# P times V in two attentions: the matmul moves the head's own 64 or 16 columns of V instead of 128

## The chip, the core and the metric

The kernel runs on one NeuronCore of a Trainium2 chip. The metric is the device time of one execution in microseconds (us); ns are nanoseconds. Both kernels compute the same function of the same inputs.

## What is computed

Eight layers follow each other on a residual of 4 batches x 512 tokens x 256 channels: a Mamba layer, a mixture of experts, a rotary attention, the same mixture, an attention with sinks, a second mixture, a latent attention, and the second mixture again. Cut to the three attentions, where `ln` is a layer norm:

```python
x = x + rotary(ln(x))   # 16 heads of 16, causal:           att = softmax(q k^T / 4);   y = att v
x = x + sinks(ln(x))    # 32 query heads, 8 kv heads of 64, softmax over all 512 keys and one
                        # sink logit, keys of the last 64 positions masked;             y = w v
x = x + latent(ln(x))   # 16 heads of 128 over one latent k, causal, v is k itself;     y = att k
```

What the change touches is the product `att v` (P times V) of the rotary and the sinks attention.

## The kernel before

One function, `attention`, writes all three attentions from a description `a`: `a.D` is the head size (16 rotary, 64 sinks, 128 latent), `a.HG` = 4 the query heads of a group, `a.G` the groups (4, 8, 4), `KW` the width of all V heads (256, 512, 128). Names of tiles begin with `ra_`, `sa_` and `la_`.

The work of a group in a batch is 16 units `u`: four query tiles of 128 tokens, `qt = u // 4`, times four heads `hh = u % 4`. Where the attention is causal a unit has `nb = qt + 1` key blocks of 128 (1 to 4, on the average 2.5); in the sinks attention `nb` is 4 always. A unit goes through these steps:

- `score` (L1771, L1775): K^T times Q into a bank `SC`, and a mask added by one more matmul (`mask`, `identb`, in bf16). There is one L1775 per unit, so its starts count units.
- maximum (L2065, VectorE), its negative (L2070 or L2074), exponential (L1939, ScalarE).
- `turn_p` (L1785): TensorE transposes P, 128 columns a block, into a bank `PT`.
- `keep_p` (L2084 on VectorE for even units, L1950 on ScalarE for odd ones): the bank is copied to `pT`.
- `values` (L1802): for each key block one fp32 matmul with the block of `pT` (128 x 128) as the weights and a slice of `vv` as what moves through the array, into the head's slice of 128 columns of a bank `OB`.
- `normalize` (L2106, VectorE), once for four units: reads the first `a.D` columns of each head's slice.

An fp32 matmul shows as two LDWEIGHTS and two MATMUL records in the trace, an fp32 transpose as one of each. In the sinks attention the scores are fp32r, two matmuls a unit.

The order on TensorE is written out by hand: in step `u` it does `turn_p(u-2)`, `score(u)`, `values(u-3)`. In step 1 of every four it also transposes the queries of the next tile (L1756, after a one-column L1705 in the rotary attention) and projects those of the one after (L1745); step 0 of every four first waits for the copy of the transposed queries by ScalarE (L1915, and L1930 in the sinks attention). The rotary L1745 is an fp32 matmul that moves 4 x 16 = 64 columns over 128 x 128 weights (`ra_xb`). A batch is: keys and values (L1718, L1735), the groups, the output product (L1865, L1875).

V lies in `vv` with `VW = KW + P - a.D` columns a block, so that 128 columns can be read from the last head on; the added columns are zeroed once by `pool.memset` (L1676). Of the 128 columns of the result only the first `a.D` are read; the others come from the next heads' V.

Of the kernel before, what the change touches and what calls it, by code (L numbers as in the profile page):

```python
# [19 lines left out]
P = 128  # L20
# [3 lines left out]
TPB = SEQ // P  # L24
# [14 lines left out]
class Counter:  # L39
# [6 lines left out]
    def at(self, n):  # L46
        return self.base + n
# [1466 lines left out]
def attention(c, a):  # L1514
# [8 lines left out]
    nc, t = c.nc, c.t  # L1523
    QW = a.HG * a.D
    KW = a.KH * a.D
    HD = a.H * a.D
    OC = HD // P
    UN = TPB * a.HG
    with ExitStack() as s:
        sb = lambda name, shape, dt=F32: s.enter_context(nc.sbuf_tensor(f"{a.name}_{name}", shape, dt))  # L1530
# [6 lines left out]
        inc = lambda n: (sig[n].sem, 1)  # L1537
# [27 lines left out]
        if a.latent:  # L1565
            b_q, b_k, b_o = sb("b_q", [P, HD]), sb("b_k", [P, KW]), sb("b_o", [P, D_MODEL])
# [33 lines left out]
        kT = [sb(f"kT{w}", [WR, a.KH * SEQ], F32R) for w in range(NC)]  # L1600


        VW = KW + P - a.D
        vv = sb("v", [P, TPB * VW])
        qst = sb("qst", [P, a.HG * WR], PART)
        qT = [[sb(f"qT{u}_{w}", [WR, a.HG * P], F32R) for w in range(PASSES)] for u in range(2)]
        pr = [sb(f"p{u}", [P, SEQ]) for u in range(4)]
# [8 lines left out]
        SC, PT, OB, QB, TQ = c.banks[0:2], c.banks[2:4], c.banks[4:6], c.banks[6], c.banks[7]  # L1616
# [1 line left out]
        KG = a.KH // a.KT  # L1618
        ROUNDS = -(-OC // 4)
        RW = min(4, OC)  # L1620
        CONSTS = 7 + (VW > KW)

        AHEAD, TURN = (1, 1) if a.parts else (3, 1)

# [28 lines left out]
        with nc.Block() as block:  # L1653

            @block.gpsimd
            def _(pool):
                pool.memset(mask[:, :], 0.0).then_inc(*inc("made"))
                pool.memset(identb[:, :], 0.0).then_inc(*inc("made"))
                pool.wait_ge(*at("made", 2))
                pool.affine_select(out=identb[:, :], in_=identb[:, :], compare_op=ALU.not_equal, fill=1.0,  # L1660
                                   base=0, pattern=[[-1, P]], channel_multiplier=1).then_inc(*inc("made"))
                if a.window:

                    pool.memset(mask[:, :], NEG).then_inc(*inc("made"))
                    pool.wait_ge(*at("made", 4))
                    pool.affine_select(out=mask[:, :], in_=mask[:, :], compare_op=ALU.is_ge, fill=0.0,
                                       base=P, pattern=[[-1, MW]], channel_multiplier=1).then_inc(*inc("made"))
                    pool.wait_ge(*at("made", 5))
                    pool.affine_select(out=mask[:, :], in_=mask[:, :], compare_op=ALU.is_gt, fill=0.0,
                                       base=a.window - P, pattern=[[1, MW]], channel_multiplier=-1) \  # L1670
                        .then_inc(*inc("made"))
                else:
                    pool.affine_select(out=mask[:, :], in_=mask[:, :], compare_op=ALU.is_ge, fill=NEG,
                                       base=0, pattern=[[-1, P]], channel_multiplier=1).then_inc(sig["made"].sem, 3)
                if VW > KW:
                    pool.memset(vv[:, :].rearrange("p (t n) -> p t n", t=TPB)[:, :, KW:], 0.0) \  # L1676
                        .then_inc(*inc("made"))
                pool.memset(xnT[:, KC * TOKENS:], 0.0).then_inc(*inc("made"))
                if a.parts:

                    pool.wait_ge(*at("loaded", 16 * len(LOADS)))
                    with pool.Fori(0, BATCH) as b:
                        with pool.Fori(0, a.G) as g:
                            for qt in range(TPB):
                                t = (b * a.G + g) * TPB + qt
                                st = Steps(pool, sig["own_q"])
                                st.loop = t * 3
                                pool.wait_ge(*at("qraw", t + 1))
                                st.then(rotate(st, a, qrot[:, :], qraw[:, :], a.HG, qt, cos, sin, t3, t4))
                                pool.wait_ge(*at("qturned", t))  # L1690
                                parts = qst[:, :].rearrange("p (h s r d) -> p h s r d", r=REP, s=2, d=a.D)
                                split(st, parts[:, :, 0, :, :], parts[:, :, 1, :, :], qrot[:, :], a.HG) \
                                    .then_inc(*inc("qput"))

            @block.tensor
            def _(pe):
                pe.wait_ge(*at("made", CONSTS))
                pe.wait_ge(*at("loaded", 16 * len(LOADS)))
# [8 lines left out]
                with pe.Fori(0, BATCH) as b:  # L1707
# [16 lines left out]
                    def turn_keys(i):  # L1724
                        n = b * TPB + i
                        pe.wait_ge(*at("kput", n + 1))
                        for m in range(KG):

                            pe.wait_ge(*at(KEPT, n * KG + max(m - 1, 0)))
                            carry_wait(PT[m % 2])  # L1730
                            for hh in range(a.KT):
                                h = m * a.KT + hh
                                src = vv[:, i * VW:i * VW + KW] if a.latent else \
                                    kst[:, h * WR:(h + 1) * WR].bitcast(F32)
                                last = pe.transpose(PT[m % 2][0:WR, hh * P:(hh + 1) * P], src, c.ident[:, :])  # L1735
                            last.then_inc(*inc("kturned"))
# [52 lines left out]
                    def values(I, g, u, before, earliest):  # L1789
                        qt, hh = divmod(u, a.HG)  # L1790
                        pe.wait_ge(*kept(I, u, before))
                        if hh == 0 and not earliest:
                            pe.wait_ge(*at("normed", I * TPB + ((u - before) // a.HG - 1)))
                        nb = keys(qt) // P
                        for kb in range(nb):
                            heads = a.HG if a.KH == a.H else 1
                            if a.latent:
                                v = vv[:, kb * VW:(kb + 1) * VW]
                            else:
                                v = vv[:, bass.ds(g * (heads * a.D) + (kb * VW + hh % heads * a.D  # L1800
                                                                       - before // UN * heads * a.D), P)]
                            last = pe.matmul(OB[qt % 2][:, hh * P:(hh + 1) * P],  # L1802
                                             pT[u % 2][:, kb * P:(kb + 1) * P], v,
                                             start=(kb == 0), stop=(kb == nb - 1))
                        last.then_inc(*inc("summed"))
# [83 lines left out]
            def _(act):  # L1889
# [5 lines left out]

                act.wait_ge(*at("made", CONSTS))
                keep_x(0)
# [4 lines left out]
                with act.Fori(0, BATCH) as b:  # L1902
# [75 lines left out]
                    for i in range(TPB):  # L1978
                        if not a.latent:
                            act.wait_ge(*at("kvp", b * TPB + i + 1))  # L1980
                            act.activation(vv[:, i * VW:i * VW + KW], OB[i % 2][:, 0:KW],
                                           ACT.Copy).then_inc(*inc("vput"))
                        if i >= 1:
                            keep_keys(i - 1)
                        if i == 1:
                            fetch_q(b * (a.G * TPB))
# [13 lines left out]
            def _(dve):  # L2000
# [27 lines left out]
                with dve.Fori(0, BATCH) as b:  # L2028
# [9 lines left out]
                    def put_keys(i):  # L2038
                        n = b * TPB + i
                        dve.wait_ge(*at("kvp", n + 1))  # L2040
                        if a.latent:
                            dve.tensor_tensor(vv[:, i * VW:i * VW + KW], SC[i % 2][:, 0:KW], b_k[:, :], ALU.add) \
                               .then_inc(*inc("kput"))
                        else:
                            dve.wait_ge(*at("kturned", n * KG))
                            st = Steps(dve, sig["own_k"])
                            st.loop = n * 3
                            st.then(rotate(st, a, krot[:, :], SC[i % 2][:, 0:KW], a.KH, i,
                                           cos, sin, t1, t2))
                            parts = kst[:, :].rearrange("p (h r s d) -> p h r s d", r=REP, s=2, d=a.D)  # L2050
                            split(st, parts[:, :, :, 0, :], parts[:, :, :, 1, :], krot[:, :], a.KH) \
                                .then_inc(*inc("kput"))
# [97 lines left out]
                    for qt in range(TPB):  # L2150
                        n = b * TPB + qt
# [13 lines left out]
        for n, v in dict(  # L2165
                loaded=16 * len(LOADS), made=CONSTS, whigh=3 if a.cut else 0, wlow=3 if a.cut else 0,
                xlow=BATCH + 1 if a.cut else 0, klow=TILES if a.latent else 0, qlow=NI * TPB if a.latent else 0,
# [96 lines left out]
```

## Time and profile before

| what | value |
|---|---|
| median of 2 runs | 4829.0 us (4824.67 to 4833.33) |
| profiled execution | 4832.96 us, of which 4831.2 us from the first to the last instruction |
| mean granted TensorE clock | 0.869 of 2.4 GHz |
| TensorE, VectorE, ScalarE, GpSimd busy | 79%, 56%, 45%, 33% |
| rotary attention | from about 980 to 1600 us |
| sinks attention | from about 2016 to 3500 us |
| latent attention | from about 3850 to 4500 us |

PE is the matmuls of TensorE, PEld its loads of weights, DVE VectorE, ACT ScalarE, POOL GpSimd. PEclk is the granted TensorE clock as a share of 2.4 GHz; it stands at 1.0 (2.4 GHz) or at 0.5 (1.2 GHz), and a value between is a mean over a stretch with both. A row of the timeline gives the start, the time from the first start to the last end of xN instructions, the engine, the line and the tiles. The end of a matmul is modelled and lies well behind the time at which the next one can start, so the time that a matmul takes from its neighbours is read from starts. In the same way "busy" of PE hides waits that are shorter than this tail.

### The profile page before, as it was taken

The numbers are of one execution on the slowest core, as the hardware profiler recorded it, in microseconds if no ns is written. First come the engines' busy times: TensorE is split into PE (matmuls) and PEld (weight loads), VectorE is DVE, ScalarE is ACT, GpSimd is POOL, SyncE is SP. The second block draws the span as 40 slices with busy tenths as digits, with TensorE's granted clock in tenths as the row PEclk, the third lists the DMA queues.
The fourth block names the chain that finished last, engine by engine and source line by source line (L and its number), as shares of the span: only waits on it lengthen the run. The fifth ranks groups of instructions, "written<-read, shape, count | busy, mean of one in ns | idle before, by whom it ended". The sixth has DMA issues, their size and how long they took to land. (4 is left out here: it accounts for less than half of the span.)

```text
span 4831.2 us, 85299 instructions
## 1 busy us (share of the span) xinstructions
PE 3839.2 (79%) x24186; PEld 3073.7 (64%) x24187; DVE 2728.5 (56%) x6679; ACT 2175.6 (45%) x5347; POOL 1575.5 (33%) x2593
## 2 busy tenths in 40 slices
PE   7799759188899487299989989989937399999554
PEld 3455547166777365178878878878825288888543
DVE  5799566444454655456456456456453375566362
ACT  3789314044555133166566556556502254444211
POOL 0499425521223145433133133133226200000055
PEclk9799869688999588599999999999957699999766
DMA  2111315400000335200000000000043400000424
GB/s 73 31 46 48 138 46 138 102 5 1 1 0 0 123 111 122 92 1 0 1 1 0 1 1 0 1 1 0 1 154 58 104 1 1 2 1 1 154 35 99
DMA packets 112289, 205.06 MB, mean 42 GB/s; under 512 B 24048, under 2 KB 85744, under 8 KB 110144
## 3 DMA queue, kind: packets, MB, share of 16 engines
q1 hardware_dynamic: 78224, 131.89, 8.1%
q0 software_dynamic: 33792, 69.83, 6.7%
q8 instruction: 135, 2.21, 0.2%
q14 instruction: 138, 1.13, 0.1%
HBM read 146.93 MB, written 54.53 MB: 42 GB/s over the span
## 5 line engine op out<-in xcount | busy, mean ns | idle before, releaser
L2065 DVE TENSOR_REDUCE sa_mx<-bank 128x1 f32<-128x512 f32 x512 | 352.8, 689 | 438.4 <-PE bank L1775 438.3
L1802 PE MATMUL bank<-sa_v,sa_pT 128*128 (+1 forms) x4096 | 550.3, 277 | 0.7
L1939 ACT ACTIVATE sa_p<-bank,sa_nm 128x512 f32<-128x512 f32 x512 | 351.6, 687 | 384.5 <-DVE sa_nm L2070 382.7
L1802 PEld LDWEIGHTS bank<-sa_v,sa_pT 128*128 128x128 f32 x4096 | 501.4, 193 | 4.2 <-issue 3.1
L239 PE MATMUL bank<-ident,ln_stage 128*128 128x128 f32 x256 | 77.1, 434 | 412.4 <-DVE ln_stage L215 408.5
L1255 POOL DMA_INDIRECT ex_xr<-scratch_rows,mo_token x288 | 286.3, 994 | 349.5 <-issue 310.6
L1502 POOL TENSOR_TENSOR sa_t<-sa_qraw,sa_cos 128x64 f32<-128x64 f32 x256 | 83.6, 327 | 959.1 <-ACT sa_qraw L1924 959.1
L597 POOL TENSOR_TENSOR sc_h<-sc_h,sc_c 128x512 f32<-128x512 f32 x256 | 327.0, 1290 | 200.3 <-DVE sc_h L634 192.3
L1771 PE MATMUL bank<-sa_kT,sa_qT 128*128 (+1 forms) x1024 | 367.2, 440 | 2.8 <-ACT sa_qT L1930 2.8
L1785 PE MATMUL bank<-ident,sa_p 128*128 128x128 f32 x2048 | 313.1, 276 | 53.5 <-ACT sa_qT L1930 51.6
L634 DVE TENSOR_TENSOR_SCAN sc_h<-sc_da,bank 128x512 f32<-128x512 f32 x256 | 311.1, 1220 | 40.1 <-ACT sc_da L577 25.3
L239 PEld LDWEIGHTS bank<-ident,ln_stage 128*128 128x128 f32 x256 | 44.0, 228 | 432.1 <-DVE ln_stage L215 428.0
L1321 PE MATMUL bank<-mo_w_gu,ex_xT 128*128 (+2 forms) x1152 | 309.9, 397 | 2.7 <-ACT ex_xT L1369 1.7
L1369 ACT ACTIVATE ex_xT<-bank 128x256 f32<-128x256 f32 (+1 forms) x288 | 105.1, 365 | 419.0 <-PE bank L1303 397.8
L1785 PEld LDWEIGHTS bank<-ident,sa_p 128*128 128x128 f32 x2048 | 234.4, 141 | 74.7 <-issue 72.2
L672 PE MATMUL bank<-sc_h,ident 128*128 128x512 f32 x512 | 262.7, 595 | 0.1
L2065 DVE TENSOR_REDUCE ra_mx<-bank 128x1 f32<-128x128 f32 (+3 forms) x256 | 125.4, 490 | 216.3 <-PE bank L1775 216.0
L1169 POOL IOTA rg_m<- 128x48 f32 x2 | 0.3, 171 | 735.0 <-POOLq L1653 679.4
L1321 PEld LDWEIGHTS bank<-mo_w_gu,ex_xT 128*128 128x128 f32 (+1 forms) x1152 | 207.5, 202 | 19.7 <-issue 5.5
L1939 ACT ACTIVATE la_p<-bank,la_nm 128x128 f32<-128x128 f32 (+3 forms) x256 | 135.1, 528 | 187.7 <-DVE la_nm L2074 187.7
L1939 ACT ACTIVATE ra_p<-bank,ra_nm 128x128 f32<-128x128 f32 (+3 forms) x256 | 134.9, 527 | 186.4 <-DVE ra_nm L2074 186.4
L660 PEld LDWEIGHTS bank<-ident,sc_db 128*128 128x128 f32 x1024 | 129.2, 142 | 137.2 <-issue 84.0
(346 smaller groups left out, 10044.2 us busy)
## 6 DMA issues: line engine op xcount, KB each, us to landing
scratch_ys<-ex_yo SPq DMA_DIRECT2D x192, 128.0 KB
mo_w_gu<-in_w_gu SPq DMA_DIRECT2D x2, 9216.0 KB, 26.3
sc_c<-scratch_c SPq DMA_DIRECT2D x64, 256.0 KB, 3.1
mo_w_dn<-in_w_dn SPq DMA_DIRECT2D x2, 4608.0 KB, 47.9
mo_w_dn<-in_w_dn SPq DMA_DIRECT2D x2, 4096.0 KB, 33.6
scratch_rows<-ln_stage POOLq DMA_DIRECT2D x64, 128.0 KB, 5.3
ex_xr<-scratch_rows,mo_token POOLq DMA_INDIRECT x288
scratch_sum<-zeros SPq DMA_DIRECT2D x2, 2176.0 KB, 10.4
```

Source lines behind the costliest of these rows:

```text
L239: last = pe.transpose(c.banks[i % 2][:, k * P:(k + 1) * P], src[:, k * P:(k + 1) * P], c.ident[:, :])
L597: pool.tensor_tensor(h, h, C[u], ALU.mult).then_inc(used.sem, 1)
L634: dve.tensor_tensor_scan(H[v % 4], DA[v % 3], TB[v % 3][:, :], 0.0, ALU.mult, ALU.add) \
L660: last = pe.transpose(TB[v % 3][:, i * P:(i + 1) * P], DB[phase % TRIO][:, at:at + P], c.ident[:, :])
L672: pe.matmul(ACC[k][:, :], c.ident[:, :], H[(phase * BLK + k) % 4], start=False, stop=last) \
L1255: pool.indirect_dma_start(xr[u][:, :], None, rows, bass.IndirectOffsetOnAxis(ap=token[:, i:i + 1], axis=0), bounds_check=rows.shape[0] - 1 ...
L1321: last = pe.matmul(GUB[u][0:ROWS, 0:GU], xT[u][:, k * ROWS:(k + 1) * ROWS], w_gu[:, bass.ds(e * (KC * GU) + k * GU, GU)], start=(k == 0), ...
L1771: pe.matmul(bank[:, 0:keys(qt)], qT[qt % 2][q_][:, hh * P:(hh + 1) * P], key, start=(w == 0), stop=False)
L1785: last = pe.transpose(PT[u % 2][:, kb * P:(kb + 1) * P], pr[u % 4][:, kb * P:(kb + 1) * P], c.ident[:, :])
L1802: last = pe.matmul(OB[qt % 2][:, hh * P:(hh + 1) * P], pT[u % 2][:, kb * P:(kb + 1) * P], v, start=(kb == 0), stop=(kb == nb - 1))
L1939: act.activation(pr[u % 4][:, 0:keys(qt)], SC[u % 2][:, 0:keys(qt)], ACT.Exp, bias=nm[:, col:col + 1], scale=a.scale, accum_out=rs[:, col: ...
L2065: dve.reduce_max(mx[:, col:col + 1], SC[u % 2][:, 0:keys(qt)], AX) \
```

## The change

The pad of `vv` goes away: a block is `KW` columns, `made` counts one constant less, and the memset is gone. The matmul of `values` moves `a.D` columns of `vv` and writes `a.D` columns of the head's slice. For the latent attention `a.D` is 128 and `VW` was equal to `KW`, so nothing changes there. Everything else is the same, in the same order.

```diff
-        VW = KW + P - a.D
-        vv = sb("v", [P, TPB * VW])
+        vv = sb("v", [P, TPB * KW])
-        CONSTS = 7 + (VW > KW)
+        CONSTS = 7
-                if VW > KW:
-                    pool.memset(vv[:, :].rearrange("p (t n) -> p t n", t=TPB)[:, :, KW:], 0.0) \
-                        .then_inc(*inc("made"))
                             if a.latent:
-                                v = vv[:, kb * VW:(kb + 1) * VW]
+                                v = vv[:, kb * KW:(kb + 1) * KW]
                             else:
-                                v = vv[:, bass.ds(g * (heads * a.D) + (kb * VW + hh % heads * a.D
-                                                                       - before // UN * heads * a.D), P)]
-                            last = pe.matmul(OB[qt % 2][:, hh * P:(hh + 1) * P],
+                                v = vv[:, bass.ds(g * (heads * a.D) + (kb * KW + hh % heads * a.D
+                                                                       - before // UN * heads * a.D), a.D)]
+                            last = pe.matmul(OB[qt % 2][:, hh * P:hh * P + a.D],
                                              pT[u % 2][:, kb * P:(kb + 1) * P], v,
                                              start=(kb == 0), stop=(kb == nb - 1))
-                            act.activation(vv[:, i * VW:i * VW + KW], OB[i % 2][:, 0:KW],
+                            act.activation(vv[:, i * KW:(i + 1) * KW], OB[i % 2][:, 0:KW],
```

## Rows read from the trace of the kernel before

**Rows 1.** Sums by stretch: rotary, then sinks attention. Span, busy PE PEld DVE ACT POOL, PEclk
```profile
980.00:1600.00 620.00, 555.53 (x3564) 432.50 (x3563) 297.71 (x940) 306.65 (x887) 150.33 (x518) 0.89 0.02 6
2016.00:3500.00 1484.00, 1376.74 (x10004) 1178.61 (x10005) 820.83 (x1963) 880.29 (x2046) 445.90 (x1156) 0.98 0.00 1
```

**Rows 2.** Rotary timeline at the full clock: weight loads, then matmuls
```profile
1049.91 0.53 PEld L1745 LDWEIGHTS bank<-ra_w_q,ra_xb 128*128 128x128 f32 x4
1051.20 0.98 PEld L1802 LDWEIGHTS bank<-ra_v,ra_pT 128*128 128x128 f32 x8
...
1050.02 0.56 PE L1745 MATMUL bank<-ra_w_q,ra_xb 128*128 x4
1050.41 0.60 PE L1785 MATMUL bank<-ident,ra_p 128*128 128x128 f32 x4
```

**Rows 3.** Sinks timeline of PE, from a period of four units (2599.71 to 2609.20)
```profile
2599.71 0.63 PE L1785 MATMUL bank<-ident,sa_p 128*128 128x128 f32 x4 [0.38 <-ACT sa_qT L1930]
...
2605.64 0.28 PE L1775 MATMUL bank<-sa_mask,sa_identb 128*128 128x256 bf16 x1
2605.77 1.06 PE L1802 MATMUL bank<-sa_v,sa_pT 128*128 x8
...
2609.20 0.30 PE L1785 MATMUL bank<-ident,sa_p 128*128 128x128 f32 x1 [0.45 <-ACT sa_qT L1930]
```

**Rows 4.** The same stretch on DVE and ACT
```profile
2605.97 0.69 DVE L2065 TENSOR_REDUCE sa_mx<-bank 128x1 f32<-128x512 f32 x1 [1.04 <-PE bank L1775]
...
2607.77 1.19 ACT L1930 ACTIVATE sa_qT<-bank 64x512 fp32r<-64x512 f32 x2
```

**Rows 5.** Sums by stretch: four starts of the rotary groups, clock at half
```profile
1018.80:1035.90 17.10, 16.87 (x69) 12.32 (x67) 5.79 (x22) 7.11 (x25) 4.51 (x16) 0.50 0.00 1
1169.00:1196.30 27.30, 26.95 (x106) 19.87 (x107) 9.27 (x32) 10.01 (x33) 6.83 (x25) 0.50 0.00 1
1322.60:1346.50 23.90, 23.68 (x94) 17.43 (x93) 8.62 (x31) 9.35 (x31) 6.76 (x24) 0.50 0.00 0
1472.80:1489.90 17.10, 16.06 (x65) 11.75 (x66) 5.78 (x22) 6.38 (x23) 5.18 (x18) 0.50 0.00 0
```

**Rows 6.** The same eight units (4 to 11), in two groups of one batch
```profile
1174.94:1195.42 20.48, 20.48 (x82) 15.16 (x82) 7.18 (x24) 7.77 (x24) 4.84 (x17) 0.50 0.00 0
1210.16:1222.20 12.04, 11.98 (x81) 8.88 (x81) 7.06 (x24) 7.45 (x26) 4.64 (x17) 1.00 0.01 2
```

**Rows 7.** A whole group of 16 units, from its first mask to the next's
```profile
1203.70:1230.06 26.36, 26.30 (x190) 20.70 (x189) 14.75 (x48) 15.06 (x49) 9.02 (x32) 1.00 0.01 2
```

**Rows 8.** First to last mask of the rotary groups, sum of the four batches
```profile
sum 441.90, PE 431.39 PEld 332.78 DVE 228.31 ACT 233.81 POOL 134.84; mean PE 107.85 PEld 83.19 DVE 57.08 ACT 58.45 POOL 33.71
```

**Rows 9.** Rotary timeline of PE at half the clock
```profile
1183.77 1.17 PE L1802 MATMUL bank<-ra_v,ra_pT 128*128 128x128 f32 x4
1184.73 0.21 PE L1705 MATMUL bank<-zeros 128*128 128x1 bf16 x1
...
1185.63 0.95 PE L1745 MATMUL bank<-ra_w_q,ra_xb 128*128 128x64 f32 x4
1186.38 0.64 PE L1785 MATMUL bank<-ident,ra_p 128*128 128x128 f32 x2
```

**Rows 10.** Narrow products of the router (L903, 48 columns move), all engines
```profile
3603.00:3642.00 39.00, 22.15 (x129) 21.22 (x130) 31.36 (x30) 0.00 (x0) 12.54 (x11) 0.50 0.01 3
3616.13 2.75 PE L903 MATMUL bank<-mo_hid,mo_row_hot 128*96 128x48 f32 x16 [0.89 <-DVE mo_row_hot L1015]
```

**Rows 11.** Sinks, batch 0: last stretch at half the clock, then the first L1802
```profile
2049.70:2063.30 13.60, 8.98 (x36) 7.50 (x37) 2.10 (x5) 4.73 (x9) 3.42 (x9) 0.50 0.00 0
2065.93 1.11 PE L1802 MATMUL bank<-sa_v,sa_pT 128*128 128x128 f32 x8
```

**Rows 12.** Sinks, first to last mask of the groups, sum of the four batches
```profile
sum 1210.90, PE 1144.92 PEld 979.95 DVE 740.09 ACT 783.01 POOL 424.47; mean PE 286.23 PEld 244.99 DVE 185.02 ACT 195.75 POOL 106.12
```

**Rows 13.** The zeroing of the pad
```profile
L1676 POOL MEMSET sa_v<- x1: 311/311/311, 2016.5 to 2016.5; 128x256 f32 x1
```

More of the change, by code:

```diff
@@ L1732, in turn_keys @@
                                 h = m * a.KT + hh
-                                src = vv[:, i * VW:i * VW + KW] if a.latent else \
+                                src = vv[:, i * KW:(i + 1) * KW] if a.latent else \
                                     kst[:, h * WR:(h + 1) * WR].bitcast(F32)
@@ L2041, in put_keys @@
                         if a.latent:
-                            dve.tensor_tensor(vv[:, i * VW:i * VW + KW], SC[i % 2][:, 0:KW], b_k[:, :], ALU.add) \
+                            dve.tensor_tensor(vv[:, i * KW:(i + 1) * KW], SC[i % 2][:, 0:KW], b_k[:, :], ALU.add) \
                                .then_inc(*inc("kput"))
```

## The prediction

> **What bounds the kernel now.** I read the sums by stretch first, because what a product is worth is decided in its own stage. In both attentions that the change touches TensorE is shown busy for nine tenths of the time, VectorE and ScalarE for half to six tenths; the reader should see that the granted clock differs: 0.89 in the rotary stage, 0.98 in the sinks stage [rows 1]. So a nanosecond off TensorE's stream is worth something, and so is its clock. I then read the timeline of TensorE by starts, weight loads beside matmuls, since the modelled ends hide what a matmul really takes; then what releases TensorE in a period of the sinks units; last, the stretches in which the clock stands at half.
>
> **What a narrower move saves.** The stage already holds an fp32 product with the form that the sinks product gets: L1745, 128x128 weights and 64 moving columns. At the full clock its four loads take 0.53 us and a single one 0.19, so they start (0.53 - 0.19) / 3 = 113 ns apart; the eight loads of L1802, with 128 moving columns, start (0.98 - 0.19) / 7 = 113 ns apart [rows 2]. The load of 128 columns of weights sets the pace in both; the matmul of 128 columns only just fills it. What half the columns give is one step at the end of a run: L1745's four records occupy 1050.02 to 1050.41, 0.39 us, where four steps of 0.111 would be 0.445. So a run of `values` gets shorter by about 0.055 us, whatever its length, and 16 columns give hardly more, as the loads remain. Bounds: nothing, and 0.1 us a run.
>
> In the sinks attention there are 512 such runs. A period of four units lasts 2609.20 - 2599.71 = 9.49 us and begins with TensorE idle for 0.4 us until ScalarE has copied the queries (L1930) [rows 3]. What is late there is a chain that TensorE does not pace: the third unit's mask at 2605.64, its maximum at 2605.97, exponential, the two copies of L1930 from 2607.77 on, TensorE again at 2609.20 [rows 3, 4]. The two runs inside this chain only lengthen the idle time; the two ahead of it pull everything forward. 256 x 0.055 = 14 us gained of 1210.9 [rows 12], with bounds of 0 and 28. In the rotary attention, at today's clock, most units have no such wait: 256 runs give at most 14 us, say 11. The memset of the pad takes 0.31 us on GpSimd at 2016.5, some 49 us before the first use of V, while the weights load; it is worth nothing [rows 11, 13]. VectorE and ScalarE read and write what they did; no DMA changes. The latent attention is untouched.
>
> **What it does to the clock.** Each batch of the rotary attention enters its groups at half the clock and stays there for 17.1, 27.3, 23.9 and 17.1 us, 85.4 in all. In these stretches TensorE is shown busy nearly throughout (26.95 of 27.30 us) [rows 5]. They hold the query tiles with few key blocks; the clock rises only near the tiles with three and four blocks, where runs of six and eight wide products follow each other. These are exactly the products that the change thins out: their loads remain, the columns moved fall from 128 to 16. A product of that kind stands in the trace: the router's L903 moves 48 columns per load in bursts of 16 with 0.9 us between, TensorE is busy for 22.15 of 39.0 us, and the clock is at half throughout [rows 10]; the gaps make this a weaker witness than the rotary stretches. I therefore expect that after the change nothing inside the rotary groups raises the clock, and that all four batches run their groups at 1.2 GHz.
>
> By the Trainium skill, "TensorE: Matmul & The Clock Gate", the section "Why this matters for your kernels", one keeps TensorE continuously busy to be at the full clock. By that rule the changed stream, still without gaps, would keep it, and the sum would be that of the first rival below; the trace has 27.3 busy us at half the clock against it.
>
> The price comes from rows at either level. Units 4 to 11 of a group take 20.48 us at half and 12.04 at full clock, 1.70 times [rows 6]. The other eight units of a 16-unit group take 26.36 - 12.04 = 14.32 at full clock [rows 6, 7]; they hold 52 of the 80 value records, which double, so I take 1.8 times, 25.8 (bounds 1.7 and 2.0: 24.3 and 28.6). A group at half the clock with wide products would be 46.3 us. The narrow product takes its step back at this level too: L1802's four records take 0.96 us (1183.77 to 1184.73), L1745's four 0.75 [rows 9], of which some 0.107 a run I count as the width's, 1.7 for 16. That leaves 44.6, or 18.2 more than today.
>
> - Groups 2 to 4 of each batch: 12 x 18.2 = 218, less about 6, as each last group has only 15 intervals: 212.
> - First groups: 441.9 [rows 8] less twelve groups of 26.36 (plus 12 for those last intervals) is about 137; 85 of it is at half already and some 10 lies ahead; the other 42 grow by 0.85, that is 36, less 5 saved in 52 runs: 31.
> - The tail of each batch (last transposes, products, output product) starts at half until its 256-column products raise the clock: an estimate of 3 us, four times: 12.
>
> Rotary: +255 us. Would the sinks attention follow? There each unit has four key blocks and fp32r scores of 512 columns for each head, twice, and the moving width stays 64. The clock is at half until 2063.30, the first L1802 comes at 2065.93 [rows 11]: it rises before any product of V has run, so the change can't take that rise away. I leave it at full.
>
> Sum: +255 - 14 = +241 on the profiled execution, 4833 + 241 = 5074. The median of the runs is 4 us below that execution: 5070.
>
> **Rivals.**
>
> - The clock stays as it is. Then only the 14 and 11 us are left: 4829 - 25 = 4804, the same within 2%. For it: TensorE's stream stays dense, and today the clock is 1.0 over most of the groups. Against it: the busy stretches at half [rows 5]. This is the one on the other side: it decides from the point at which the thin units still raise the clock in the first group of a batch.
> - The product goes at the pace of its columns. By the Trainium skill, the same page, "Back-to-back issue gap", an isolated matmul takes its columns over the clock plus some 2.5 ns. As a mechanism of this kernel: 0.055 in place of 0.111 us a record in the sinks (8 x 0.055 = 0.44 a run, 256 runs on the path: -113 us) and about 0.02 in the rotary groups (1280 records x 0.09 = -115): 4600, faster. Rows 2 speak against it outright.
> - The clock alternates in the rotary groups; half of the loss: 4829 + 115 = 4945, slower.
> - The sinks attention falls to half as well. Its groups would go from 1211 us to 1.7 to 1.8 times that [rows 6, 12]: about +900 more, near 5970. Against it: the rise before the first product, and wide scores in every unit.
>
> That the matmul does not become narrower in the program at all belongs to the first rival (4829).
>
> **How the numbers follow.** Half the clock throughout the rotary groups 0.80; clock as today 0.12; alternating 0.03; sinks too 0.03; pace of the columns 0.02. The likeliest alone spans 5020 to 5125: factor 1.7 for all units takes 24 us off, 2.0 puts 46 on, and the sinks term adds 14 either way. The range reaches a little below that, to 5000, and leaves the other cases, 0.20, out; it ends at 5130. About 2% is what a measurement of this kernel can tell from no change. Slower by more: 0.80 + 0.03 + 0.03 = 0.86. Within 2%: 0.12. Faster: 0.02.
>
> **What would show it.** In the profile after: PEclk in the sums of the rotary groups at 0.50 (the whole stage stands at 0.89 now), a group of 16 units near 44.6 us, L1802's loads still 113 ns apart at the full clock in the sinks stage and 214 ns at half in the rotary one; a period of sinks units of 9.38 us with the idle time before L1785 grown by about 0.1; stages after the rotary one of unchanged length. The prediction is wrong if the rotary groups still show a clock near 0.9, and its sum is wrong if the eight units 4 to 11 take much else than 20.48 less 0.9 us.

## The result and the profile after

| | before | after |
|---|---|---|
| median (2 runs each) | 4829.0 us | 5077.88 us (5076.94 to 5078.82) |
| ratio | | 1.051, 95% interval 1.0484 to 1.0536 |
| profiled execution | 4832.96 us | 5076.94 us |
| mean granted TensorE clock | 0.869 | 0.813 |
| rotary groups, first to last mask, four batches | 441.9 us | 677.1 us |
| sinks groups, the same | 1210.9 us | 1205.7 us |
| latent groups, one batch | 114.1 us | 114.1 us |

The change makes the kernel 5.1% slower, by 244 us between the two profiled executions. The next rows are the sums by stretch of the changed kernel: the rotary groups of the first batch and the sum of all four, then the same eight units and the same whole group as in [rows 6, 7], in the second batch:

```profile
1009.46:1178.72 169.26, 166.91 (x698) 128.39 (x698) 58.26 (x187) 62.03 (x186) 33.61 (x120) 0.51 0.00 1
...
sum 677.14, PE 667.72 PEld 513.59 DVE 233.01 ACT 248.12 POOL 134.47; mean PE 166.93 PEld 128.40 DVE 58.25 ACT 62.03 POOL 33.62
...
1277.16:1296.63 19.47, 19.47 (x82) 14.28 (x82) 7.26 (x24) 7.79 (x24) 4.51 (x16) 0.50 0.00 0
1265.93:1310.41 44.48, 44.48 (x189) 34.73 (x189) 15.09 (x48) 16.11 (x48) 9.02 (x32) 0.50 0.00 0
```

The number of TensorE instructions is that of before (698 in the batch shown), and the other engines run as many as before; the clock column reads 0.50 to 0.51 where a group stood at 1.0 [rows 7]. TensorE is shown busy for the whole of a group that takes 1.69 times as long: the busy share tells nothing of the loss.

The timeline of the weight loads in the changed kernel, first a rotary unit with four key blocks, then a sinks unit:

```profile
1307.23 1.81 PEld L1798 LDWEIGHTS bank<-ra_v,ra_pT 128*128 128x128 f32 x8
...
2855.03 0.98 PEld L1798 LDWEIGHTS bank<-sa_v,sa_pT 128*128 128x128 f32 x8
```

(L1798 is L1802 of before.) In the sinks stage the eight loads take 0.98 us as they did with 128 moving columns [rows 2], though the matmuls between them move 64; in the rotary stage they take 1.81 us with 16. The loads set the pace and go with the clock. That it is the loads, and not a fixed time for each fp32 record, can be read from the router in the kernel before. Its products [rows 10] load 96 columns of weights in place of 128:

```profile
3614.84 0.28 PEld L903 LDWEIGHTS bank<-mo_hid,mo_row_hot 128*96 128x96 f32 x1
3616.13 2.63 PEld L903 LDWEIGHTS bank<-mo_hid,mo_row_hot 128*96 128x96 f32 x16 [1.01 <-DVE mo_row_hot L1015]
```

A single one of these loads takes 0.28 us, so the sixteen start (2.63 - 0.28) / 15 = 0.157 us apart at half the clock, about three quarters of the 0.213 of loads of 128 columns (the run of TensorE alone, below).

### The profile page after: what moved, and what is told of

It reads as the page before. It is cut to its first block and busy times, and to the rows that moved or that the text cites. A ratio compares the mean times of both kernels' runs of the same rounds, so it can differ in the third digit from the quotient of the medians.

```text
span 5075.2 us, 85297 instructions
## 1 busy us (share of the span) xinstructions
PE 4085.0 (80%) x24186; PEld 3266.5 (64%) x24187; DVE 2737.6 (54%) x6679; ACT 2190.1 (43%) x5347; POOL 1574.6 (31%) x2591
## 5 line engine op out<-in xcount | busy, mean ns | idle before, releaser
L1798 PE MATMUL bank<-sa_v,sa_pT 128*128 (+1 forms) x4096 | 529.9, 272 | 4.2 <-issue 1.0
L1798 PEld LDWEIGHTS bank<-sa_v,sa_pT 128*128 128x128 f32 x4096 | 501.3, 193 | 13.0 <-issue 6.4
L1798 PE MATMUL bank<-ra_v,ra_pT 128*128 128x16 f32 (+1 forms) x1280 | 304.9, 367 | 0.0
L1798 PEld LDWEIGHTS bank<-ra_v,ra_pT 128*128 128x128 f32 x1280 | 298.6, 330 | 0.0
L1502 POOL TENSOR_TENSOR ra_t<-ra_qraw,ra_cos 128x32 f32<-128x32 f32 x128 | 34.0, 266 | 659.4 <-ACT ra_qraw L1920 659.4
```

What stands on the lines that cost most here:

```text
L1502: eng.tensor_tensor(small(t1)[:, :, half, :], v(src)[:, :, half, 0:R], c_, ALU.mult)
L1798: last = pe.matmul(OB[qt % 2][:, hh * P:hh * P + a.D], pT[u % 2][:, kb * P:(kb + 1) * P], v, start=(kb == 0), stop=(kb == nb - 1))
```

## The experiments

Kernel times below are medians; each comparison is with runs of the kernel before on the same chip, which had medians of 4824 to 4830 us in these sessions. A time without an interval comes from one execution. Rows of single stretches come from the profiled execution of each kernel.

### Which half of the change

```diff
-        VW = KW + P - a.D
+        MOVE = {'ra': 128, 'sa': 64, 'la': 128}[a.name]   # the second run: 'ra': 16, 'sa': 128
+        VW = KW + MOVE - a.D
...
-                                                                       - before // UN * heads * a.D), P)]
-                            last = pe.matmul(OB[qt % 2][:, hh * P:(hh + 1) * P],
+                                                                       - before // UN * heads * a.D), MOVE)]
+                            last = pe.matmul(OB[qt % 2][:, hh * P:hh * P + MOVE],
```

> Only the sinks product is narrowed to 64 columns; the rotary product moves 128 as in the kernel before. Theory (the loss is the clock of the rotary groups, set off by the 16-column product): the rotary groups keep their clock and a group of 16 units takes 26.4 us; the sinks groups take 37.9 us as in the changed kernel against 38.1 before; in all 4829 - 5 = 4824 us. Rival (the loss comes from the change as a whole, for instance from the layout of V without its pad or from both products): the rotary stage is slow here too, above 5000 us.

> Only the rotary product is narrowed, to 16 columns; the sinks product moves 128. Theory: the whole loss is here: PEclk 0.50 in the rotary groups, 44.5 us a group, and 5078 + 5 = 5083 us. Rival: as for the other half, if the loss is shared by both parts this one is clearly below 5050 us.

Measured: 4820.9 us with only the sinks product narrowed (ratio 0.9991, 0.9982 to 1.0001), 5086.8 us with only the rotary one (1.0539, 1.0522 to 1.0555). The sums by stretch give the rotary stage of the first kernel, at a clock of 0.90, and the rotary groups of the second in its first batch:

```profile
980.00:1590.00 610.00, 549.26 (x3552) 427.51 (x3552) 292.06 (x923) 303.46 (x880) 150.31 (x518) 0.90 0.01 3
1012.22:1181.51 169.29, 166.94 (x698) 128.43 (x698) 58.23 (x187) 61.91 (x186) 33.64 (x120) 0.51 0.00 1
```

The whole loss belongs to the 16-column product; the sinks half is worth some 5 us, and the interval of its ratio just takes in no change.

### The disputed cost by itself

All layers are left out here, and the output is the input, so this kernel does not compute the function. Only TensorE works, with fp32 matmuls over 128x128 weights that are loaded anew for each, and it waits for nothing.

```diff
+            def run16(k):                       # and the same with 128, 96 and 64 columns
+                for i in range(k):
+                    pe.matmul(c.banks[i % 2][:, 0:16], c.x[:, i % 2 * P:(i % 2 + 1) * P],
+                              c.x[:, 512:512 + 16], start=True, stop=True)
+            for other in (run96, run64, run16, turn):     # turn: transposes
+                run128(150)
+                other(150)
+            run128(100)
```

> All layers are left out; the output is the input. TensorE alone runs 150 fp32 matmuls each of 96, 64 and 16 moving columns and 150 transposes, each after 150 of 128 columns, all with 128x128 weights loaded anew for each, without any wait. Theory (the load of 128 columns of weights sets the pace, the moved columns set the clock): every width has its records 0.111 us apart as long as the clock is 1.0; 96 columns keep the clock at 1.0; 16 columns lose it soon after they begin and then go at 0.214 us a record, although the engine never waits; 64 columns are open. Rival A (columns set the pace): 64 columns at 0.056 us, 16 at about 0.02 us a record. Rival B (a busy engine keeps its clock): 1.0 for every width to the end.

The timeline of its matmuls, merged by line (300 records are 150 matmuls; the form gives the moving columns), and the sums by stretch from the 64 columns on (busy PE, busy PEld, POOL, PEclk):

```profile
44.82 33.64 PE L2192 MATMUL bank<-residual 128*128 128x96 f32 x300
78.29 33.69 PE L2187 MATMUL bank<-residual 128*128 128x128 f32 x300
111.82 33.61 PE L2197 MATMUL bank<-residual 128*128 128x64 f32 x300
145.26 33.72 PE L2187 MATMUL bank<-residual 128*128 128x128 f32 x300
178.82 59.51 PE L2202 MATMUL bank<-residual 128*128 128x16 f32 x300
```
```profile
112.00:145.00 33.00, 33.00 (x298) 33.00 (x298) 0.00 (x0) 1.00 0.00 1
146.00:178.00 32.00, 32.00 (x289) 32.00 (x288) 0.00 (x0) 1.00 0.01 2
184.00:238.00 54.00, 54.00 (x255) 54.00 (x255) 0.00 (x0) 0.50 0.00 1
```

The blocks of 300 records start 33.4 to 33.6 us apart, 0.112 a record, with 128, 96 and 64 moving columns alike: a narrower move gives nothing inside a run. With 16 columns the first 43 records are 0.112 us apart too. Then, 5 us after they begin and without any wait, the clock falls to half and stays there to their end, and the records are 0.213 us apart. It comes back once matmuls of 128 columns follow. Rival A and rival B fall. 64 columns keep a clock that was high when they began.

### Can thin units hold the clock, or only not raise it?

In the first group of each batch the rotary product moves 128 columns, in the other three 16.

```diff
-                    def values(I, g, u, before, earliest):
+                    def values(I, g, u, before, earliest, cols=MOVE):
...
-                                values(I, g, u - 3, 0, first and u < 3 + 2 * a.HG)
+                                values(I, g, u - 3, 0, first and u < 3 + 2 * a.HG, P if first else MOVE)
```

> Rotary product with 128 columns in the first group of each batch and 16 in the other three; sinks 64. The clock therefore rises in the first group as before. Theory 1 (16-column units can neither raise nor hold the clock): within the second group the clock falls to half and the later groups take 44.5 us: about 5078 - 4 x 8 = 5045 us. Theory 2 (they cannot raise it, but hold it once it is high): the later groups take 26.4 - 0.9 = 25.5 us at PEclk 1.0, in all about 4815 us.

Measured 5029 us. Sums by stretch in the second batch, whose groups begin at 1209.32: the first group at its start, its end together with the start of the second, and the thin groups:

```profile
1210.00:1239.00 29.00, 27.09 (x106) 20.01 (x107) 9.46 (x33) 10.49 (x35) 8.18 (x29) 0.53 0.00 0
1239.00:1252.00 13.00, 13.00 (x103) 10.88 (x102) 6.58 (x21) 7.68 (x22) 3.78 (x15) 1.00 0.00 0
1255.00:1369.00 114.00, 114.00 (x475) 87.56 (x474) 40.48 (x127) 41.86 (x124) 20.37 (x72) 0.50 0.00 0
```

The clock rises in the first group as before and falls again within the second, which takes 36.5 to 39.5 us in the four batches; the third takes 44.48 us in all of them. Theory 1: the thin units neither raise nor hold it. The kernel is 16 us below the 5045 that the theory gave, because it counted only the first groups: these take 26.0 us less than in the changed kernel, and the second groups, which keep the high clock for a part, another 23.4.

### How thin is too thin here

> Both products move 64 columns (in the rotary attention three heads' columns too many). In the run of TensorE alone 64 columns kept a clock that was already high. Theory (in the groups the clock has to rise from half, and needs the wide runs of the tiles with four key blocks for it): with 64 columns it does not rise, a group takes 44.5 us and the whole some 5075 us. Rival (only the nearly empty 16-column product is too thin): the clock rises as before, a group takes 25.5 us, the whole 4815 us.

> As the run before, with 96 columns in the rotary product. It asks between which widths the clock is lost. If it rises somewhere in the first group: 25.5 us a group and 4810 to 4840 us; if not, some 5075 us. The theory gives no side; what it excludes is a value that does not come from one of these two states or a mix of them by batch.

The edit is that of the first experiment with `'ra': 64` and `'ra': 96`, sinks 64. Measured: 5078 us with 64 columns, 4883 us with 96. Sums by stretch of the rotary groups: first batch with 64 columns, then the four batches with 96:

```profile
1009.82:1179.86 170.04, 167.46 (x698) 129.04 (x698) 58.24 (x187) 61.91 (x186) 33.81 (x120) 0.51 0.00 1
```
```profile
1006.09:1144.91 138.82, 135.91 (x699) 105.18 (x698) 57.45 (x186) 59.62 (x185) 33.81 (x120) 0.68 0.00 1
1184.47:1304.02 119.55, 116.78 (x699) 90.27 (x698) 57.12 (x186) 58.71 (x184) 33.66 (x120) 0.81 0.00 0
1346.83:1486.07 139.24, 136.52 (x698) 105.50 (x697) 57.44 (x186) 59.60 (x184) 33.73 (x120) 0.67 0.00 1
1526.65:1639.65 113.00, 110.22 (x698) 85.08 (x697) 57.02 (x186) 58.61 (x184) 33.66 (x120) 0.86 0.00 0
```

64 columns, which kept a high clock in the run of TensorE alone, do not raise it in any of the four batches here, and four times the columns of the change buy nothing (the groups take 44.8 us against 44.5). With 96 the clock rises in every batch, but at different places: twice in the third group, once in the second, once in the first. The four batches do the same work and last from 113 to 139 us. My expected range for a rise (4810 to 4840) took it for granted in the first group; 4883 is the mix by batch that the text also named.

### Work added to get the clock back

`fill` writes into a bank that TensorE owns at the time; its results are overwritten. Ahead of `kput` it comes after a wait for the bank; this wait stands in all three attentions, also where `fill` is given nothing to do. The second kernel has no filler in `turn_p` and moves 128 columns in the rotary product.

```diff
+                def fill(n, bank):
+                    for _ in range(n if a.name == 'ra' else 0):
+                        pe.matmul(bank[:, 0:256], c.zeros[:, 0:P], c.zeros[:, 0:256], start=True, stop=True)
...
                     def turn_keys(i):
                         n = b * TPB + i
+                        pe.wait_ge(*at(KEPT, n * KG))
+                        fill(20 if i == TPB - 1 else 6, PT[0])
                         pe.wait_ge(*at("kput", n + 1))
...
                     def turn_p(I, u, before, earliest):
...
+                        fill(3, PT[u % 2])
...
                             score(g, u)
+                            fill(16 if first and u == 0 else 4 if first and u < 4 else 0, OB[1])
```

> The changed kernel (16 and 64 columns) with filler in the rotary attention: bf16 matmuls of zeros with 256 columns, three ahead of each unit's transposes, and 4 to 20 at the places of the keys stage and of the first units where TensorE waits. It only adds work. Theory (the loss is the clock, and moving columns keep it): the clock stays or rises to 1.0, a group takes 25.5 + 16 x 3 x 0.11 = 30.7 us in place of 44.5, and the kernel gets faster by some 4 x 4 x 13 = 200 us, about 4880 us. Rival (the loss is something else in the narrow product): the filler adds 16 x 3 x 0.22 = 10 us a group, about 5240 us.

> Sinks 64 columns, rotary 128 as before, with filler (bf16 zeros, 256 columns) only where TensorE waits: ahead of the wait for the rotated keys (6, and 20 at the last tile) and after the scores of the first units of a batch (16, then 4 each). Theory: the clock stays high into the groups, so the 17 to 27 us at half at the start of each batch go; first groups take 25 to 26 us in place of 32 to 37, together 25 to 30 us less than the run with only the sinks product narrowed (4821): 4795 us. Rival (the clock at the start depends on something else, or the filler delays the keys as much as it saves): 4820 us or more.

Measured: 4928 us for the first, 150 us less than the changed kernel (5078), by adding some 250 matmuls a batch to it. Sums by stretch: four batches, and two stretches of 50 us in its third and fourth batch:

```profile
1006.37:1156.88 150.51, 150.13 (x913) 117.38 (x912) 58.11 (x187) 60.11 (x186) 33.65 (x120) 0.74 0.00 1
1194.69:1323.82 129.13, 128.75 (x913) 101.98 (x912) 57.93 (x187) 59.21 (x186) 33.67 (x120) 0.88 0.00 1
1364.20:1493.34 129.14, 128.76 (x912) 101.89 (x911) 57.92 (x187) 59.22 (x186) 33.65 (x120) 0.88 0.00 1
1532.33:1685.95 153.62, 153.23 (x913) 119.68 (x913) 58.12 (x187) 60.12 (x186) 33.65 (x120) 0.72 0.00 1
1450.00:1500.00 50.00, 49.74 (x394) 40.52 (x393) 25.00 (x76) 25.94 (x76) 9.87 (x34) 1.00 0.00 1
1600.00:1650.00 50.00, 50.00 (x221) 38.70 (x221) 14.57 (x48) 14.36 (x45) 9.01 (x32) 0.50 0.00 0
```

Groups at the high clock take 29.7 us (30.7 expected), groups at half 48.5 to 49, in one program. The first groups, which follow the filler at the waits, are all at the high clock; later the clock falls to half in the second or third group of every batch, for 31 to 85 us. So the gain is smaller than expected (4880 us), because three fillers a unit hold the clock only part of the time. The direction settles the cause: a loss from anything else in the narrow product would have grown with the added work.

The second: 4776.5 us, ratio 0.9899 (0.988 to 0.9917). The rotary groups of its four batches:

```profile
1007.24:1110.42 103.18, 102.20 (x727) 79.28 (x726) 56.93 (x186) 58.02 (x184) 33.78 (x120) 1.00 0.00 1
...
sum 412.78, PE 408.86 PEld 317.16 DVE 227.65 ACT 232.13 POOL 135.18; mean PE 102.21 PEld 79.29 DVE 56.91 ACT 58.03 POOL 33.80
```

The batches took 108.3 to 113.0 us in the kernel before, 441.9 in sum [rows 8]; now they take 103.2, all four alike, because their first groups no longer begin at half [rows 5] and last 27.2 us (25 to 26 expected) in place of 32 to 37. The gaps between batches shrink by some 2 us each as well. What the groups lost to the clock at their start was there to be had in the kernel before.

The kernel is 19 us faster than the 4795 expected, and not all of that is the clock. Against the run with only the sinks product narrowed, the profiled execution is 45.4 us shorter: 21.5 in the rotary groups and 12.4 in the gaps between them, 4.9 ahead of the first group, and 9.0 in the three gaps between the batches of the latent attention, where this kernel has no filler; the other stages took 2.4 back. These gaps are 150.5 to 152.3 us in sum in the kernels that have the new wait but no filler there, and 159.3 to 160.5 in all without the edit. The wait, or the place of the code that it moves, is what differs; no run separates the two. So what the filler gave through the clock in the rotary attention is some 34 us, 0.7% of the kernel, and the wait may have a share in the gaps there too.

### Where the sinks gain went

The forecast gain was 14 us, the measured one 5. The intervals between masks in a period of four sinks units were 3.07, 1.92, 1.92 and 2.57 us before, and are 3.02, 1.87, 1.87 and 2.69 us after: the first three give 0.05 us each, as forecast. The last one holds the idle time. Had the chain kept its length it would have grown by the 0.05 of the third interval; it grew by 0.11 (the medians are 2.574 and 2.688), and of the 0.11 us that a period was to gain only 0.05 are left. The chain, from the third unit's mask to the return of TensorE, grew from 3.56 to 3.61 us. The timeline shows where; GpSimd and VectorE in the kernel before, then in the changed one:

```profile
2606.63 0.29 POOL L1505 COPY sa_qrot<-sa_qraw 128x128 f32<-128x128 f32 x1
2606.70 0.24 DVE L2070 SCALAR_TENSOR_TENSOR sa_nm<-sa_mx,sa_negsink 128x1 f32<-128x1 f32 x1
```
```profile
2856.07 0.29 POOL L1505 COPY sa_qrot<-sa_qraw 128x128 f32<-128x128 f32 x1
2856.08 0.29 DVE L2066 SCALAR_TENSOR_TENSOR sa_nm<-sa_mx,sa_negsink 128x1 f32<-128x1 f32 x1
```

The negated maximum takes 0.16 us in most other units (in 24 to 26 of the 128 fourth units it takes up to 0.65, in both kernels). In 117 of the 128 third units, in both kernels, it is lengthened as here, and it lasts until some 14 ns after the end of GpSimd's copy. The copy is timed by the queries that ScalarE hands over (L1924) after the exponential of the unit before. Before, that hand-over began with the third unit's mask (2605.64 both); in the changed kernel it begins 0.05 us after it (2855.08 and 2855.03), because the third mask follows the second by 1.92 us in the one and 1.87 in the other, while the exponential follows the second mask by 1.24 in both. So VectorE reaches its instruction at the same distance from the mask, and is held 0.05 us longer.

```diff
-                            dve.scalar_tensor_tensor(out=nm[:, col:col + 1], in0=mx[:, col:col + 1],
-                                                     scalar=-a.scale, in1=negsink[:, bass.ds(g * a.HG + hh, 1)],
-                                                     op0=ALU.mult, op1=ALU.min).then_inc(*inc("negged"))
+                            dve.tensor_scalar(nm[:, col:col + 1], mx[:, col:col + 1], -a.scale,
+                                              negsink[:, bass.ds(g * a.HG + hh, 1)],
+                                              ALU.mult, ALU.min).then_inc(*inc("negged"))
```

> Rotary 128 columns, sinks 64, and one more edit: the negated maximum of the sinks attention (VectorE) reads the negated sink as a scalar operand in place of a second tensor operand. In the traces this instruction ends 14 ns after GpSimd's copy of the rotated queries in the third unit of each four, 0.24 us long with the wide and 0.29 with the narrow product, against 0.16 elsewhere. Theory (the hold by GpSimd eats what the narrow product saves ahead of it): with a scalar operand it is 0.16 everywhere, a period of four sinks units takes 9.42 - 0.13 = 9.29 us, and the kernel 4821 - 17 = 4804 us. Rival (the hold is a chance of order, or the form makes no difference): 4821 us.

> The same edit with 128 columns in both products. Theory: the hold was 0.08 us here, so 4827 - 10 = 4817 us, and the narrow sinks product is then worth 2 x 0.055 us a period as forecast, 13 us between this run and the one before. Rival (the narrow product is worth only the 5 us measured without the edit): both runs within 6 us of each other.

Measured: 4818.9 us (0.9969, 0.9958 to 0.998) with 64 columns, 4827.1 us (0.9997, 0.9987 to 1.0008) with 128. The instruction, by its tile (minimum, median, maximum in ns), in the kernel before and in the narrow run:

```profile
L2070 DVE SCALAR_TENSOR_TENSOR sa_nm<-sa_mx,sa_negsink x512: 158/160/642, 2057.7 to 3469.9; 128x1 f32<-128x1 f32 x171
```
```profile
L2071 DVE TENSOR_SCALAR sa_nm<-sa_mx,sa_negsink x512: 212/214/217, 2062.0 to 3457.8; 128x1 f32<-128x1 f32 x171
```

and the sinks groups of both, narrow then wide, first to last mask of four batches:

```profile
sum 1194.00, PE 1119.20 PEld 963.35 DVE 756.13 ACT 780.93 POOL 424.09; mean PE 279.80 PEld 240.84 DVE 189.03 ACT 195.23 POOL 106.02
```
```profile
sum 1206.89, PE 1141.67 PEld 977.47 DVE 750.92 ACT 781.03 POOL 424.28; mean PE 285.42 PEld 244.37 DVE 187.73 ACT 195.26 POOL 106.07
```

The expected 0.16 us everywhere was wrong: the scalar form costs 0.214 us each time, but it is never held. So both totals lie above what was expected (4804 and 4817). The difference is what the experiment was for: 1206.9 - 1194.0 = 12.9 us in the sinks groups, as forecast for the narrow product (13), where it is 5.2 with the hold. The medians are only 8.2 us apart, closer to the rival's 6 than to 13; they also hold the rotary first groups, which in these two profiled executions took 32.4 to 37.1 us, so the sinks groups decide here and not the kernel times.

### A version that beats both

> The filler at the waits of the keys stage and of the first units in all three attentions, the sinks product with 64 columns, the rotary one with 128, and the scalar operand. Theory: 4776 of the run with filler in the rotary attention alone, less 17 for the scalar operand, less a few us for the starts of the sinks and latent batches: 4755 us. Rival (where the clock already rises before the products, filler only delays the scores): 4776 us or more.

> As the run before without the filler in the latent attention, whose groups took 116.3 us a batch with it against 114.1 without and whose starts were 2 to 5 us later. Theory (only that filler ate the gain of the rest): 4779 - 4 x 2.1 - 3 x 3.5 = 4760 us, 0.986 of the kernel before. Rival (the time is lost elsewhere): 4775 us or more.

Both are the sinks product with 64 columns, the rotary one with 128, the scalar operand, and the filler at the waits; in the first in all three attentions, in the second not in the latent one. Measured: 4782.4 us (0.9908, 0.9894 to 0.9922) where 4755 was expected, then 4757.9 us (0.9854, 0.9834 to 0.9875), as expected (4760). In the latent attention the filler stood in the way: its groups took 116.3 us a batch in place of 114.1. Without it the profiled execution is 19.6 us shorter, 8.5 in these groups, 8.4 in the three gaps between them (those of the wait told of above) and 3.0 ahead of the first. In the second kernel the sinks groups take 1191.0 us (1210.9 before) and the rotary ones 412.5. It is 1.5% faster than the kernel before and 6% faster than the changed one; some 9 of its 67 us against the kernel before lie in the latent gaps, whose cause is open.

## Why the prediction was right

**The clock.** Forecast: all rotary groups at half. Measured: PEclk 0.50 to 0.51 in all four batches. The experiments show the cause from five sides: one half of the change alone, the product alone without any wait, thin groups behind a high clock, widths between, and work added. What I argued from the busy stretches at half [rows 5] held.

**The price of a group.** Forecast 44.6 us, measured 44.48. The eight units of [rows 6] take 19.47 us; 20.48 less 0.9 was forecast. The factor 1.8 for the other eight was chosen between 1.7 and 2.0; measured, they take 44.48 - 19.47 = 25.01 us, and with the narrow product's 0.9 added back 25.9 against my 25.8. The first groups take 41.4 us each, 27.8 more than before in sum (31 forecast).

**The sum.** +241 was forecast and +244.0 measured, and part of that closeness is luck. From the first rotary mask to the end of the last output product of that attention the stage grew by 257.1 us, where +255 was forecast. The groups gave 235.2 of it (243 forecast). The tails, from a batch's last mask to the end of its output product, took 15.4 to 15.9 us in place of 9.7, which is 24.0 in four: the estimate of 12 was too low by half. The stretches between tail and next batch gave 2.4 back. The sinks groups gained 5.2 (14 forecast). That would make +252. But the rotary stage also began 6.2 us earlier in the profiled execution of the changed kernel, and no layer ahead of it was changed: in the kernels without filler its first mask comes anywhere from 1006.1 to 1015.7 us. The last 2 us lie in the other stages. The kernel before scatters as well: its four first groups take 137.6 us in sum in the execution that the forecast was built on, and 130.2 to 142.1 in the three other kernels with the wide rotary product and no filler.

**The pace.** Forecast: loads 113 ns apart at any width. Measured: 0.98 us for eight loads in the sinks stage, 0.112 us a record at 128, 96 and 64 columns in the run of TensorE alone, and 0.213 at half the clock (214 ns forecast). The 0.055 us a run came out as 0.05 between masks.

**The sinks term** was mis-sized too, and for a cause of its own: 5 us where 14 were forecast. I took the chain that TensorE does not pace as fixed. It has an instruction in it that waits for another engine, and lengthened as the rest became shorter. The row for it was in the trace (0.24 us against a usual 0.16), and I had passed over it.

**The rise in the sinks attention** before the first product of V held: in the changed kernel the clock is at full 1.1 to 2.4 us ahead of the first product of V of each batch, and PEclk is 0.99 in the groups before and after.

## What to carry to other kernels

Where each fp32 matmul loads 128 columns of weights, as here, moving fewer columns saved one step at the end of a run and no more; look for the pace in the starts of the loads, not in the width of the move. The columns that seem wasted may be what keeps TensorE's clock: before thinning out a stream, look at the granted clock in the thinnest stretches of the same stage. Here the answer already stood there at both levels, with its price. A busy share near 100% is no sign of a high clock. Throw-away matmuls where TensorE waits anyway, ahead of a stage that began at half, gained some 0.7% here; in the latent attention, whose groups stood at the full clock without them, they cost 2.1 us a batch.

## What the runs showed of the hardware

- A stream of 16-column fp32 matmuls without a single wait lost the clock and stayed at 1.2 GHz to its end; in a stretch of 54 us within it TensorE is shown busy for 54.00 us. The Trainium skill, "TensorE: Matmul & The Clock Gate", section "Why this matters for your kernels", advises to keep TensorE busy continuously to get the full clock; the trace disagrees for this stream of 16 columns.
- Loads of 128 columns of fp32 weights started 112 ns apart at the full clock and 213 at half, loads of 96 columns 157 at half. By the Trainium skill, the same page, section "LDWEIGHTS (loading the stationary operand)", a load takes its columns over 1.2 in ns, which gives an estimate of 107 ns for 128. The traces agree that the columns of the weights count; they differ in that the load goes with the granted clock, which the formula leaves out.
- Filler of bf16 zeros kept the clock at 1.00 through the rotary groups of all four batches (0.88 to 0.92 before), and brought it back within every batch of the changed kernel, whose last groups take 26.3 us in place of 39.0: the data need not differ from zero.
- One program can run the same stage at either level by batch: 113.0 to 139.2 us with 96 columns. Such a kernel has times that depend on where in the stage the clock happens to rise; with the filler all four batches were alike within 0.02 us.
- A VectorE instruction with two tensor operands in SBUF was held until the end of a GpSimd copy, 0.24 and 0.29 us long in place of 0.16; the form with one tensor operand and a scalar one took 0.214 and was not held in 512 cases. The Trainium skill, "SBUF — State Buffer", section "SBUF: two separate sides", states the rule: a VectorE instruction with two inputs in SBUF and a GpSimd instruction that reads SBUF take turns on a shared pair of ports, which the one that starts first holds to its end. The trace agrees: the copy starts first (2606.63 and 2606.70 us in the kernel before).

What stays open: why the scalar form takes 54 ns more, why the new wait, or its place, shortens the gaps of the latent attention by 9 us in sum, and what within a stage decides where the clock rises with 96 columns.
